# Moving the first batch's down products of a pair ahead of the second batch's transposes on TensorE, in place of ten filling products

## The chip, the cores and the metric

The kernel runs on one core of a Trainium2 chip. The metric is the device time of one execution in microseconds, lower being better: 1347.7 us as the median of three runs (1347.05 to 1351.74). The engines named below are TensorE (PE), VectorE (DVE), ScalarE (ACT), GpSimd (POOL) and SyncE (SP), the last of which issues most DMAs. Each engine has one instruction stream of its own and takes it in the order in which the program wrote it; the streams meet only in semaphores.

## The reference, cut to what matters

The model has two layers over 4 batches of 512 tokens of 256 values. Layer 0 is a local attention block with a feed-forward part, then a mixture of experts with a shared expert. Layer 1 is a slot attention of three rounds with a second mixture of experts. The change is in the shared expert and the routing of layer 0:

```
# layer 0, after the attention block; xn is the normalised residual x
logits = xn @ w_router.T                     # 8 experts
weight, idx = top_k(softmax(logits), 2)      # two experts a token
...
sh = square(relu(xn @ ws1.T))                # 256 -> 512: "up"
shared_out = sh @ ws2.T                      # 512 -> 256: "down"
return shared_out + moe_out                  # added to x through a gate
```

## The kernel before, in words

**Stages.** The first stage (layer 0 up to its experts) works on the four batches in two pairs. Inside a pair the batches 0 and 1 (then 2 and 3) are interleaved; the suffix of a step's name is the batch's place in its pair, and with it the half of PSUM (four banks each) and the set of buffers that it uses. After both pairs come the grouped experts of layer 0, then slot attention, then the experts of layer 1.

**What sets the order.** `ORDER_A` (lines 48 to 56) lists, for each engine by itself, the steps of one pair. `stages_a` (line 292) yields them for pair 0 and pair 1; a small replacement changes the beginning of pair 0 only. Nothing reorders them. At the end of a pair the steps are:

- `xnT`: PE turns (transposes) the normalised rows `S2` into banks 2 and 3 (`turn_xn`, line 1474; 8 transposes, L1461). ACT copies them to the high part of `RT` (L924), DVE makes the low part (L1103).
- `logits`: PE multiplies by the router's weights (6 products, L206 to L208; three products stand for one multiplication of split numbers). ACT's `lt` copies the logits out (L928), PE's `lt` turns them (L1487), and DVE's `logits` is `choose` (line 1105): the largest, the softmax, the best two experts. In the middle of `choose` DVE waits for the exponential on ACT (L932); that is ACT's step `logits`.
- `upA`, `upB`: PE computes the four blocks of 128 hidden rows of the shared expert. ACT takes each through Relu (L980) and Square (L982), and the square counts `sh_sq`.
- `rank`: PE sums how many earlier tokens chose each expert (L1493, L1494), DVE's `place` (line 1153) turns that into the row of destination (`dest`, L1166).
- `down`: PE waits for all four squares of the batch, then makes 16 products into banks 2 and 3 (L1612; each is recorded as two). DVE adds the result to `X` (L1303) and counts `batch_a`. On POOL `down` is `scatter` (line 802): eight indirect DMAs (L807) that write the tokens' rows to the experts' areas as soon as `dest` is there, and for batches 0 and 1 also the loading and splitting of expert weights (L469, L477). On SP it stores `X`, loads the next residual and, before the first of pair 1, runs `first_group_in` (line 429), which waits for the table of groups, three fills with zeros and every scatter.

ACT's list is `xnT0 lt0 upA0 logits0 upB0 xnT1 ...`; so the last two Relu and Square of the first batch stand behind the exponential of `logits0`. DVE's list is `... ffn1 logits0 xnT1 rank0 logits1 rank1 table1 down0 down1`; `ffn1` is the second normalisation chain of the second batch, which gives the rows that `xnT1` turns.

**Filling products.** `spin` (line 1464) issues products of constants into a bank that is free (L1467). Their results are read by nobody. Ten stand at the head of the second batch's `xnT`, ten at the head of `rank0`, six or four at the head of `logits`.

Of the kernel before, what the change touches and what calls it, by code (L numbers as in the profile page):

```python
# [46 lines left out]

ORDER_A = {
# [7 lines left out]
}  # L56
# [46 lines left out]
def build(nc, x, ctx_in, cols, rows, wq, wk, wv, wo, pos_bias, w1, w2, router1, m1_w1, m1_w2, ws1, ws2,  # L103
          Wq, Wk, Wv, wih, whh, router2, gate_w, up_w, down_w, down_b, out):
    top = ExitStack()
    with top:
# [5 lines left out]
        def sem(name):  # L112
            if name not in sems:
                sems[name] = top.enter_context(nc.semaphore(name))
            return sems[name]
# [78 lines left out]
        def bank(h, k):  # L194
            return PS[:, 4 * h + k, :]
# [1260 lines left out]
        def _(pe):  # L1456
# [7 lines left out]
            def spin(free, n):  # L1464

                for _ in range(n):
                    pe.matmul(free.rearrange("p (a b) -> p a b", b=P), ones_bf[:], ones_bf[:].unsqueeze(1).to_broadcast([P, TT, P]),  # L1467
                              start=True, stop=True)

            def parts(t, *at):  # L1470
                return tuple(t[(slice(None), i) + at] for i in two)
# [33 lines left out]
            for stage, n, h in stages_a("pe"):  # L1505
                if stage == "turn":
                    if n < 2:
                        spin(bank(h, 3), (16, 4)[n])
                    pe.wait_ge(sem("emb"), n + 1)
                    if n >= 2:  # L1510
                        pe.wait_ge(sem("dest"), n - 1)
                    turn(h, 0, EMB[h], "inT_ps")
                elif stage == "qk":
                    if n == 0:
                        spin(bank(0, 3), 8)
                        after(pe, "w3_split")
                    if n >= 2:
                        pe.wait_ge(sem("batch_a"), n - 1)
                    pe.wait_ge(sem("inT_lo"), n + 1)
                    for w in range(2):  # L1520
                        for c in range(C):
                            for c2 in range(C):
                                ins = product(pe, bank(h, 2 * w + c), parts(W3, w, c2, slice(c * P, (c + 1) * P)),
                                              parts(RT[h], c2), c2 == 0, c2 == C - 1)
                        ins.then_inc(sem("qk_ps"), 1)
                elif stage == "ewT":
                    pe.wait_ge(sem("ek"), 1)
                    pe.wait_ge(sem("ekv"), 1)
                    after(pe, "ew")
                    for jc in range(TT):  # L1530
                        for i in range(TT):
                            ins = pe.transpose(bank(0, jc)[:, i * P:(i + 1) * P], band[:, i, jc * P:(jc + 1) * P], ident[:])
                    once(ins, "ewT_ps")
                elif stage == "v":
                    pe.wait_ge(sem("th"), n + 1)
                    for j in range(TT):
                        for c in range(C):
                            ins = product(pe, token_banks(h, 0)[:, j], parts(RT[h], c, slice(j * P, (j + 1) * P)),
                                          parts(W3, 2, c), c == 0, c == C - 1)
                    ins.then_inc(sem("v_ps"), 1)  # L1540
                    pe.wait_ge(sem("ekT"), n + 1)
                    for j in range(TT):
                        for c in range(C):
                            ins = pe.transpose(token_banks(h, 2)[:, j, c * P:(c + 1) * P], S0[h][:, c, j * P:(j + 1) * P], ident[:])
                    ins.then_inc(sem("ek_ps"), 1)
                elif stage in ("den", "num"):

                    pe.wait_ge(sem("ek" if stage == "den" else "ekv"), n + 1)
                    if n == 0:
                        after(pe, "ewT")  # L1550
                    b, src = (2, 0) if stage == "den" else (0, 2)
                    w = HB[h][:, src:src + 2].rearrange("p b (a d) -> p (b a) d", d=D)
                    for c in range(C):
                        for j in range(TT):
                            ins = pe.matmul(bank(h, b + c), w[:, j, c * P:(c + 1) * P], EWT[:, j], start=j == 0, stop=j == TT - 1)  # L1555
                    ins.then_inc(sem(f"{stage}_ps"), 1)
                elif stage == "attn":
                    if h == 0:
                        pe.wait_ge(sem("ekv"), n + 2)
                        spin(bank(1, 0), 8)  # L1560
                    pe.wait_ge(sem("yT"), n + 1)
                    if n == 0:
                        pe.wait_ge(sem("wplain_in"), 48)
                    for j in range(TT):
                        for c in range(C):
                            ins = pe.matmul(token_banks(h, 0)[:, j], HB[h][:, 4 + c, j * P:(j + 1) * P], WO[:, c], start=c == 0, stop=c == C - 1)
                    ins.then_inc(sem("attn_ps"), 1)
                elif stage == "aT":
                    pe.wait_ge(sem("r_norm"), n + 1)
                    turn(h, 2, S2[h], "aT_ps")  # L1570
                elif stage == "hid":
                    spin(bank(h, 0), 10)
                    pe.wait_ge(sem("aT_lo"), C * (n + 1))
                    for m in range(HC):
                        if m >= 4:
                            pe.wait_ge(sem("hidden"), HC * n + m - 3)
                        for c in range(C):
                            ins = product(pe, bank(h, m % 4), parts(W1, c, slice(m * P, (m + 1) * P)), parts(RT[h], c), c == 0, c == C - 1)
                        ins.then_inc(sem("hid_ps"), 1)
                elif stage == "ffn":  # L1580
                    pe.wait_ge(sem("hidden"), HC * (n + 1))
                    for j in range(TT):
                        for m in range(HC):
                            ins = pe.matmul(token_banks(h, 0)[:, j], HB[h][:, m, j * P:(j + 1) * P], W2[:, m], start=m == 0, stop=m == HC - 1)  # L1584
                    ins.then_inc(sem("ffn_ps"), 1)
                elif stage == "xnT":
                    if h == 1:
                        spin(bank(h, 2), 10)
                    turn_xn(0, n, h, "xn")
                elif stage == "logits":  # L1590
                    spin(bank(h, 0), (6, 4)[h])
                    logits(0, n, h)
                elif stage == "lt":
                    logits_by_token(0, n, h)
                elif stage in ("upA", "upB"):
                    for f in (0, 1) if stage == "upA" else (2, 3):
                        if f >= 2:
                            pe.wait_ge(sem("sh_relu"), SC * n + f - 1)
                        for c in range(C):
                            ins = product(pe, bank(h, 2 + f % 2), parts(WS1, c, slice(f * P, (f + 1) * P)), parts(RT[h], c), c == 0, c == C - 1)  # L1600
                        ins.then_inc(sem("sh_ps"), 1)
                elif stage == "rank":
                    if h == 0:
                        spin(bank(1, 0), 10)
                    ranks(0, n, h)
                elif stage == "table":
                    table_pe(pe, 0)
                elif stage == "down":
                    pe.wait_ge(sem("sh_sq"), SC * (n + 1))
                    for j in range(TT):  # L1610
                        for f in range(SC):
                            ins = pe.matmul(token_banks(h, 2)[:, j], HB[h][:, f, j * P:(j + 1) * P], WS2[:, f], start=f == 0, stop=f == SC - 1)  # L1612
                    ins.then_inc(sem("shared_ps"), 1)
# [177 lines left out]
```

## Time and profile before

| what | value |
|---|---|
| median of three runs | 1347.7 us |
| the profiled execution: its own time | 1333.26 us |
| its span, first to last instruction | 1331.5 us |
| PE, DVE, ACT, POOL busy | 85%, 56%, 29%, 27% of the span |
| mean granted TensorE clock | 0.947 of full speed |

The first stage is the time up to about 361 us. Pair 0 ends for PE near 190.5 us, pair 1's PE work near 359 us, and the experts of layer 0 start on PE at 361.55 us. The profiled execution took 14.4 us less than the median of the timed runs; a change is read as a difference inside the profiled execution and then set on the median.

### The profile page before, as it was taken

The numbers are of one execution on the slowest core, as the hardware profiler recorded it, in microseconds if no ns is written. First come the engines' busy times: TensorE is split into PE (matmuls) and PEld (weight loads), VectorE is DVE, ScalarE is ACT, GpSimd is POOL, SyncE is SP. The second block draws the span as 40 slices with busy tenths as digits, with TensorE's granted clock in tenths as the row PEclk, the third lists the DMA queues.
The fourth block names the chain that finished last, engine by engine and source line by source line (L and its number), as shares of the span: only waits on it lengthen the run. The fifth ranks groups of instructions, "written<-read, shape, count | busy, mean of one in ns | idle before, by whom it ended". The sixth has DMA issues, their size and how long they took to land.

```text
span 1331.5 us, 17144 instructions
## 1 busy us (share of the span) xinstructions
PE 1125.3 (85%) x5915; PEld 882.1 (66%) x5915; DVE 742.3 (56%) x1778; ACT 385.3 (29%) x705; POOL 356.8 (27%) x290
## 2 busy tenths in 40 slices
PE   7989899898778677999999679999998299998930
PEld 5467676576667644787878447868784199998930
DVE  5565745657555435646555545454547366665633
ACT  3122221222234332233332333332332033332310
POOL 2423162231422161410101320101012523305235
PEclk9999999999999987999999999999999599999975
DMA  9401041000376650200000110000003854444435
GB/s 340 167 1 32 1 149 58 1 0 1 130 225 201 195 167 4 60 0 0 1 1 1 48 48 0 0 1 0 1 1 118 262 157 144 149 150 144 141 109 175
DMA packets 90833, 112.60 MB, mean 85 GB/s; under 512 B 6544, under 2 KB 76432, under 8 KB 90640
## 3 DMA queue, kind: packets, MB, share of 16 engines
q1 hardware_dynamic: 66800, 71.91, 16.7%
q0 software_dynamic: 19344, 34.35, 8.7%
q10 hardware_dynamic: 4624, 5.51, 1.3%
q8 instruction: 37, 0.61, 0.2%
q14 instruction: 28, 0.23, 0.1%
HBM read 75.04 MB, written 36.70 MB: 84 GB/s over the span
## 4 chain that ended last, share of the span: by engine, by line
PE 53%; DVE 18%; POOL 9%; issue 8%; ACT 5%; DMA 5%; SPq 2%; ACTq 0%; POOLq 0%; DVEq 0%
PE PS L206 12%; PE PS L208 10%; PE PS L207 10%; PE PS L1694 6%; PE PS L1584 4%; PE PS L1555 4%; POOL routed L807 4%; POOL HB L866 2%; DVE S L1099 2%; POOL rstd L800 2%; DVE st L1080 1%; PE PS L1461 1%; DVE SM L1379 1%; DMA outputs<-y 1%; DVE RT L1103 1%
## 5 line engine op out<-in xcount | busy, mean ns | idle before, releaser
L800 POOL TENSOR_TENSOR rstd<-ve,minus_half 128x4 f32<-128x4 f32 x40 | 40.6, 1015 | 359.3 <-DVE ve L1087 208.2
L206 PE MATMUL PS<-xt,split 128*128 128x256 f32 x412 | 121.2, 294 | 15.6 <-issue 12.5
L1467 PE MATMUL PS<-ones_bf 128*128 128x512 bf16 x433 | 114.2, 411 | 19.1 <-DMA routed<-S,dest 16.3
L207 PE MATMUL PS<-xt,split 128*128 128x256 f32 x412 | 119.2, 289 | 0.0
L208 PE MATMUL PS<-xt,split 128*128 128x256 f32 x412 | 119.0, 289 | 0.0
L477 POOL TENSOR_TENSOR split<-raw,split 128x1024 fp32r<-128x1024 f32 (+1 forms) x15 | 66.7, 4443 | 121.8 <-DMA raw<-down_w 73.1
L206 PEld LDWEIGHTS PS<-xt,split 128*128 128x128 f32 x412 | 81.7, 198 | 19.2 <-issue 14.4
L1467 PEld LDWEIGHTS PS<-ones_bf 128*128 128x128 bf16 x433 | 43.2, 105 | 75.9 <-issue 40.4
L1694 PE MATMUL PS<-VP,HB 128*128 128x257 f32 x384 | 85.8, 382 | 4.4 <-DVE VP L1392 4.4
L206 PE MATMUL PS<-split,hs 128*128 128x256 f32 x244 | 77.5, 318 | 10.5 <-DVE hs L541 8.9
L807 POOL DMA_INDIRECT routed<-S,dest x64 | 66.5, 1040 | 67.1 <-DVE dest L1166 49.3
L1694 PEld LDWEIGHTS PS<-VP,HB 128*128 128x128 f32 x384 | 72.4, 190 | 17.5 <-DVE VP L1392 7.4
L866 POOL DMA_INDIRECT HB<-outputs,source x64 | 64.0, 1000 | 68.2 <-DMA outputs<-y 49.5
L207 PEld LDWEIGHTS PS<-xt,split 128*128 128x128 f32 x412 | 81.9, 199 | 0.0
L208 PEld LDWEIGHTS PS<-xt,split 128*128 128x128 f32 x412 | 81.8, 198 | 0.0
L520 ACT ACTIVATE act<-PS,colv 128x256 f32<-128x256 f32 x84 | 39.9, 475 | 129.2 <-PE PS L208 129.2
L556 DVE SCALAR_TENSOR_TENSOR act<-PS,colv,act 128x256 f32<-128x256 f32 x84 | 40.7, 485 | 52.7 <-ACT act L520 48.3
L207 PE MATMUL PS<-split,hs 128*128 128x256 f32 x244 | 69.5, 285 | 0.0
L208 PE MATMUL PS<-split,hs 128*128 128x256 f32 x244 | 69.4, 284 | 0.0
L206 PE MATMUL PS<-HTS,WHH 128*128 128x512 f32 x144 | 60.5, 420 | 1.5 <-DVE RT L1103 1.5
L206 PEld LDWEIGHTS PS<-split,hs 128*128 128x128 f32 x244 | 46.8, 192 | 21.3 <-DVE hs L541 20.9
L1027 ACT ACTIVATE HB<-PS,SM 128x512 f32<-128x512 f32 x48 | 33.0, 688 | 94.0 <-DVE SM L1381 93.6
(305 smaller groups left out, 2730.2 us busy)
## 6 DMA issues: line engine op xcount, KB each, us to landing
xg<-routed SPq DMA_DIRECT2D x42, 256.0 KB, 2.8
outputs<-y SPq DMA_DIRECT2D x40, 256.0 KB, 2.3
outputs<-zeros SPq DMA_DIRECT2D x3, 2048.0 KB, 16.1
routed<-zeros SPq DMA_DIRECT2D x20, 256.0 KB, 3.2
split<-m_w POOLq DMA_DIRECT2D x16, 256.0 KB, 4.8
x_base<-X SPq DMA_DIRECT2D x8, 512.0 KB, 3.4
raw<-gate_w SPq DMA_DIRECT2D x8, 512.0 KB, 6.7
raw<-up_w SPq DMA_DIRECT2D x8, 512.0 KB, 8.7
```

Of the source, the lines that this page charges most:

```text
L206: pe.matmul(out_, a[1], b[0], start=first, stop=False)
L207: pe.matmul(out_, a[0], b[1], start=False, stop=False)
L208: return pe.matmul(out_, a[0], b[0], start=False, stop=last)
L477: eng.tensor_tensor(w.split[e % 2][:, 1], w.raw[:], w.split[e % 2][:, 0].bitcast(F32), ALU.subtract).then_inc(sem(f"m{m}_lo"), 1)
L556: dve.scalar_tensor_tensor(out=a[:, 1], in0=PS[:, f, 0:G], scalar=col("gate_b", e * w.fc + f), in1=a[:, 0], op0=ALU.add, op1=ALU.mult).the ...
L800: pool.tensor_tensor(rstd[h][:], ve[h][:], minus_half[:], ALU.pow).then_inc(sem("rstd_ready"), 1)
L807: pool.indirect_dma_start(out=routed[m], out_offset=bass.IndirectOffsetOnAxis(ap=dest[m][:, n, j, kk:kk + 1], axis=0), in_=S2[h][:, j], in ...
L866: pool.indirect_dma_start(out=rows_h[h][:, kk, j], out_offset=None, in_=outputs, in_offset=bass.IndirectOffsetOnAxis(ap=source[:, n, j, kk ...
L1467: pe.matmul(free.rearrange("p (a b) -> p a b", b=P), ones_bf[:], ones_bf[:].unsqueeze(1).to_broadcast([P, TT, P]), start=True, stop=True)
L1555: ins = pe.matmul(bank(h, b + c), w[:, j, c * P:(c + 1) * P], EWT[:, j], start=j == 0, stop=j == TT - 1)
L1584: ins = pe.matmul(token_banks(h, 0)[:, j], HB[h][:, m, j * P:(j + 1) * P], W2[:, m], start=m == 0, stop=m == HC - 1)
L1694: ins = pe.matmul(bank(h, j)[:, 0:D + 1], HB[h][:, m, j * P:(j + 1) * P], VP[h][:, m, 0:D + 1], start=m == 0, stop=m == TT - 1)
```

## The change

In PE's list `down0` moves from behind `table1` to behind `upB0`, that is ahead of the turn `xnT1`. In DVE's list `down0` moves from behind `table1` to behind `xnT1`, ahead of `rank0`. The ten filling products at the head of `xnT1` are removed. The lists of ACT, POOL and SP are as they were, and the same list serves both pairs.

```diff
 ORDER_A = {
     "pe": "turn0 turn1 qk0 qk1 v0 v1 den0 num0 den1 attn0 num1 attn1 aT0 hid0 aT1 hid1 ffn0 ffn1 "
-          "xnT0 logits0 upA0 lt0 upB0 xnT1 rank0 logits1 lt1 upA1 upB1 rank1 table1 down0 down1",
+          "xnT0 logits0 upA0 lt0 upB0 down0 xnT1 rank0 logits1 lt1 upA1 upB1 rank1 table1 down1",
...
     "dve": "turn0 turn1 qk0 qk1 v0 v1 den0 num0 den1 attn0 num1 norm0 aT0 attn1 norm1 aT1 in0 ctx0 in1 ctx1 ffn0 xnT0 ffn1 "
-           "logits0 xnT1 rank0 logits1 rank1 table1 down0 down1",
+           "logits0 xnT1 down0 rank0 logits1 rank1 table1 down1",
...
                 elif stage == "xnT":
-                    if h == 1:
-                        spin(bank(h, 2), 10)
                     turn_xn(0, n, h, "xn")
```

On PE, in pair 0, behind the last product of the first batch's `upB`; L1467 is a filling product, L1610 (L1612 before) a down product, L1461 a transpose of the second batch's rows:

```order
 L207 MATMUL PS<-RT,WS 128x512
 L208 MATMUL PS<-RT,WS 128x512
-L1467 MATMUL PS<-ones_bf 128x512 x10
+L1610 MATMUL PS<-WS,HB 128x256 x16
 L1461 MATMUL PS<-ident,S 128x128 x8
 L1467 MATMUL PS<-ones_bf 128x512 x10
```

The first batch's 16 down products now stand between its last up product and the transposes, and the ten filling products are gone from there.

On PE, at the end of pair 0, behind the sums of `rank1` and ahead of the next pair's transposes of `EMB`:

```order
 L1493 MATMUL PS<-rbf,tri 128x32
 L1494 MATMUL PS<-rbf,ones_bf 128x32
-L1612 MATMUL PS<-WS,HB 128x256 x32
+L1610 MATMUL PS<-WS,HB 128x256 x16
 L1461 MATMUL PS<-ident,EMB 128x128 x16
 L206 MATMUL PS<-RT,W 128x512
```

Of the 32 down products of both batches the 16 of the second one stay.

On DVE, in pair 0, between the low part of the second batch's turned rows (L1103) and `place` of the first batch (L1159 and on); L1303 adds the down products to `X`:

```order
 L1151 COPY carry<-carry 128x8
 L1103 TENSOR_TENSOR RT<-PS,RT 128x1024
+L1303 SCALAR_TENSOR_TENSOR X<-PS,tanh_g,X 128x1024
 L1159 TENSOR_TENSOR RTM<-PS,ebase 128x32
 L1162 TENSOR_TENSOR RTM<-RTM 128x32
```

The addition now stands ahead of the instructions that give `dest` of the first batch. Pair 1 shows the same three differences.

## Rows read from the trace of the kernel before

**Rows 1.** The page: busy time by engine, and the chain that ended last by engine
```profile
PE 1125.3 (85%) x5915; PEld 882.1 (66%) x5915; DVE 742.3 (56%) x1778; ACT 385.3 (29%) x705; POOL 356.8 (27%) x290
...
PE 53%; DVE 18%; POOL 9%; issue 8%; ACT 5%; DMA 5%; SPq 2%; ACTq 0%; POOLq 0%; DVEq 0%
```

**Rows 2.** The chain of waits, 130 to 410 us: start, us, what
```profile
167.13 1.14 DVE RT L1103
168.31 0.40 PE PS L206
...
176.79 13.91 PE PS L1612 x64
190.70 0.89 PE PS L1461 x8
...
336.20 1.12 POOL routed L807
...
355.38 2.44 DMA routed<-S,dest
```

**Rows 3.** Timeline of PE, end of pair 0: start, us, engine, line, what, [idle before <-releaser]
```profile
156.85 2.33 PE L1467 MATMUL PS<-ones_bf 128*128 128x512 bf16 x10
162.11 1.71 PE L1461 MATMUL PS<-ident,S 128*128 128x128 f32 x8 [2.93 <-DVE S L1099]
...
176.34 0.40 PE L208 MATMUL PS<-RT,WS 128*128 128x512 f32 x1
...
176.64 14.06 PE L1612 MATMUL PS<-WS,HB 128*128 128x256 f32 x64
190.54 1.91 PE L1461 MATMUL PS<-ident,EMB 128*128 128x128 f32 x16
```

**Rows 4.** Timeline of ACT, end of pair 0
```profile
162.42 0.23 ACT L932 ACTIVATE RTM<-RTM 128x32 f32<-128x32 f32 x1 [7.44 <-DVE RTM L1113]
...
164.31 0.63 ACT L982 ACTIVATE HB<-HB 128x512 f32<-128x512 f32 x1
164.85 1.01 ACT L924 ACTIVATE RT<-PS 128x1024 fp32r<-128x1024 f32 x1
...
177.40 0.63 ACT L982 ACTIVATE HB<-HB 128x512 f32<-128x512 f32 x1
```

**Rows 5.** Timeline of pair 1's end: PE, DVE and ACT
```profile
328.55 1.09 PE L1461 MATMUL PS<-ident,S 128*128 128x128 f32 x8 [2.92 <-DVE S L1099]
...
334.76 0.39 PE L206 MATMUL PS<-RT,rw 128*8 128x512 f32 x1 [0.35 <-DVE RT L1103]
...
334.62 0.18 DVE L1159 TENSOR_TENSOR RTM<-PS,ebase 128x32 f32<-128x32 f32 x1
...
330.75 0.63 ACT L982 ACTIVATE HB<-HB 128x512 f32<-128x512 f32 x1
```

**Rows 6.** Timeline of PE after 8 us idle, and granted clock: window, us, PE busy, PEclk
```profile
503.96 1.97 PE L1461 MATMUL PS<-ident,S 128*128 128x128 f32 x8 [8.06 <-DVE S L1099]
...
507.00:508.00 1.00, 1.00 (x6) 0.91 0.00 0
...
1061.92:1067.00 5.08, 5.08 (x24) 0.50 0.93 324
```

**Rows 7.** The DVE line of the down result; SP's wait; PE's first transposes of the experts
```profile
L1303 DVE SCALAR_TENSOR_TENSOR X<-PS,tanh_g,X x4: 1282/1284/1285, 183.8 to 359.1; 128x1024 f32<-128x1024 f32 x4
...
SPq L437 <- DMA routed<-S,dest: 3.2, 1, 3.2
...
361.55 0.63 PE L591 MATMUL PS<-ident,S 128*128 128x128 f32 x4 [2.48 <-DMA S<-routed]
```

**Rows 8.** Timeline of POOL and DVE at the start of pair 1
```profile
205.86 4.74 POOL L828 TENSOR_TENSOR EMB<-EMB,rowv 128x1024 f32<-128x1024 f32 x2
...
206.72 1.56 DVE L1239 TENSOR_TENSOR kb<-kb,colv 128x2 f32<-128x2 f32 x1
208.31 2.31 DVE L1241 TENSOR_TENSOR kb<-colv,kb 128x2 f32<-128x2 f32 x1
```

## The prediction, made before the changed kernel was run

> **What bounds the kernel now.** I read the page first. PE is busy 85% of the span and holds 53% of the chain that ended last [rows 1], so PE work that goes from the chain could pay. But these are means over stages, so the next view is the chain of waits over the first stage [rows 2]. There the two pairs end in different ways. In pair 0 the chain runs DVE (L1103), the logits at 168.31, the up products, then 13.91 us of down products, then the next pair's transposes at 190.70: the end of pair 0 is PE work. In pair 1 the chain leaves PE: from 336.20 it runs over POOL's sixteen scatters and their last landing at 357.82 (355.38 + 2.44), and the 64 records of down products are not in it. So the down products cost time in pair 0 and lie under the scatters in pair 1.
>
> Then the timeline of PE around the new place [rows 3]. Before, PE issued ten filling products at 156.85, idled 2.93 us, and turned the second batch's rows at 162.11, when DVE's normalisation gave them. About 5.3 us lie between the last up product and that turn, and a batch's down products last half of the 13.9 us from 176.64 to 190.54, 6.95 us. If they could start at 156.85, little of them would be late. So the question is when their operands are there, and that is read on ACT [rows 4]: the fourth square (L982) of the first batch ends at 164.94 (164.31 + 0.63), because ACT sat idle 7.44 us in front of the exponential L932, whose argument DVE makes only after the second batch's normalisations. In the old place nobody noticed. In pair 1 the fourth square ends at 331.38 (330.75 + 0.63) [rows 5].
>
> **The change part by part.** I sum against the profiled execution (1333.26 us, span 1331.5) and set the difference on the median, 1347.7.
>
> *The ten filling products (2.33 us in each pair) go.* They lay in PE's idle time in front of 162.11, so nothing is gained; but the idle stretch that they shortened becomes one.
>
> *down0 on PE, pair 0.* It waits for `sh_sq`, so PE stands from about 156.85 to 165.0, 8.15 us. Behind it in PE's stream are the transposes of `xnT1`, `rank0`, `logits1` and all of `upA1`, `upB1`; they wait too. The clock: after the 8.06 us idle in front of 503.96 the eight transposes took 1.97 us where the warm ones of 328.55 took 1.09, and the granted clock was at 0.50 (1.2 GHz) until it rose just behind 507.0, about 3.1 us of work; the longest stretch of that kind is 5.08 us at 0.50 [rows 5, 6]. I take 3.9 us of cold work, between the two, which does the work of half that time: +1.95 us, bounded by +1.55 and +2.55. So down0 takes 6.95 + 1.95 = 8.9 us and ends at 173.9, where before the transposes began at 162.11.
>
> From there to the logits: eight transposes warm, 0.9 us to the next instruction (190.70 has 0.89 [rows 2]); ten filling products of `rank0`, 2.33; the two sums, 0.1; four filling products, 0.93: 4.25 us, so the logits start at 178.15. The other way, ACT's copy 1.03 and DVE's low part 1.23 after the transposes, gives 177.2 and is shorter. Before, they started at 168.31: +9.85. The up products follow without a gap as before, so the last one, at 176.34, starts at 186.2.
>
> *The tail of pair 0.* down1 now is the first product after up. Its last square ended at 178.03 (177.40 + 0.63) [rows 4], hidden under down0's products; it now ends at 187.9, and PE waits some 1.4 us for it. Then 6.95 us: the next pair's transposes start at 194.85 instead of 190.54. Pair 0 costs **+4.3 us**: 9.85 later, 6.95 shorter, 1.4 of new wait.
>
> *Pair 1.* The same, from the fourth square at 331.38: down0 from 331.45 to 340.35, transposes to 341.3, ACT's copy to 342.4, DVE's low part to 343.65. In DVE's stream down0 (1.28 [rows 7]) comes next and then `place`, which began at 334.62 and now begins at 344.95: +10.3 us for the first `dest` and for the first scatter (336.20 to 346.5). The logits move from 334.76 to 344.6, +9.85, so the second batch's `dest` is 9.85 late; its eight scatters start 10.2 us after the first ones (fifteen steps from 336.20 to 355.38 are 1.28 each) and `dest` is there in time. All sixteen scatters, their landing, SP's reads of the first groups and PE's first expert transposes at 361.55 shift by 10.3. The shorter tail of PE is worth nothing: before, PE ended at 359 and idled 2.48 us [rows 7]. The table, and with it the fills, move by 9.85; SP waited 3.2 us for the last scatter after them [rows 7], so they stay hidden. Pair 1 costs **+10.3 us**. Bounds of these two terms together, from the cold stretch: 4.3 + 10.3 with -0.4 to +0.6 each.
>
> *POOL's displacement, start of pair 1.* The first scatters of pair 0 also start about 10.3 later; behind them in POOL's stream stand its split of the second expert's weights, which had some 3 us of slack in a wait for a load, and then L828. Before, L828 lay over two tiny DVE instructions, which took 1.56 and 2.31 us [rows 8] instead of about 0.16, and held ACT's exponentials. DVE's come 4.3 us later now, POOL's split and L828 some 7 us later, so the split and the first L828 lie over the two: about 2.0 + 2.3 instead of 3.9, **+0.5 us**, between -1 and +3.
>
> The Trainium skill (GPSIMD Engine Reference, section Specifications) states that GpSimd shares its SBUF interfaces with VectorE and that this hurts DVE instructions with two SBUF inputs or in a two-port mode. L1239 and L1241 have two SBUF inputs, and rows 8 agree. By that rule the moved L1303, which reads one input from PSUM, is safe wherever POOL works; its four instances spread only from 1282 to 1285 ns [rows 7], one of them beside a POOL split. By the rule the term stays near +0.5; without it I would keep the same range.
>
> *Sum:* 4.3 + 10.3 + 0.5 = +15.1 us, 1333.3 to 1348.4 in a profiled execution, and 1347.7 + 15.1 = 1362.8 in the timed runs.
>
> **The rivals.**
>
> *A, the squares are in time.* If the exponential did not hold ACT, the third and fourth squares would end near 158.3, one Relu and one Square behind the last up product. down0 would run 158.3 to 165.3 warm and the transposes be 3.2 us late. The low part was waiting for DVE's `choose` until 167.04 anyway, the logits would start near 169.5 (+1.2), and pair 0 would end 1.2 + 1.4 - 6.95 = -4.3. In pair 1 the first `dest` would be 2.8 late (1.5 from the turn, 1.28 from L1303), the total -1.5: **1346**, not slower. It decides from the point where ACT's fourth square ends before about 160. For it: 5.3 us of nearly free PE time. Against it: the 7.44 us wait of ACT [rows 4], and ACT's list is unchanged.
>
> *B, the scatters' delay is taken up before the experts.* Only pair 0 pays: 1347.7 + 4.3 = **1352**. Against it: SP waited for the last landing, and PE for SP's first read [rows 7]; the table's own shift of 9.85 less the 3.2 of slack would still leave 6.6.
>
> *C, the clock stays at 0.50 through all of down0.* Then it takes 13.9 us and each pair pays 5.0 more: 1362.8 + 10.0 = **1373**. Against it: after the same idle the clock was back after 3.1 us of work [rows 6], and down products ran densely at full speed in 176.64 to 190.54.
>
> *D, POOL's work falls worse on DVE,* for instance over three instructions that hold ACT or PE: +3 to +5 on top, **1367**. For it: rows 8 show 3.5 us lost to such a fall, and POOL's work moves by another distance than DVE's.
>
> **How the numbers follow.** Forecast 81%, A 4%, B 5%, C 4%, D 6%. The likeliest gives 1362.8, its own range 1359 to 1367 (cold stretch, POOL, and 0.1 to 0.2% of spread in the medians). The range reaches down toward B and up past D: 1355 to 1369. About 0.5%, 6.7 us, is what a measurement of this kernel can tell from no change: above 1354.4 is slower. Forecast, C and D are slower (91%); A and B are within (8%, leaving a little of B's upper side); 1% for a gain that no case shows.
>
> **What would show it.** Right: PE idle about 8 us in front of the down products in both pairs, released by ACT L982; a granted clock of 0.50 for their first 3 to 5 us; the second batch's transposes near 174 and 341; an idle of about 1.4 us in front of down1; the first scatter of pair 1 near 351 (346.5 plus pair 0's 4.3), and the first expert transposes about 15 us after 361.55. From there to the end the stretch lasts as before. Wrong: down0 starting near 158 (A); a scatter delay that doesn't reach the experts (B); down0 records still 0.44 us apart at its end (C); long tiny instructions on DVE near 211 with PE waiting behind them (D).

## The result

The changed kernel took 1356.9 us (median of 4 executions) against 1347.4 us for the kernel before on the same chip: a ratio of 1.0077, 95% interval 1.0056 to 1.0098, that is 7.5 to 13.2 us slower with its middle at +10.4. Timed a second time on another chip it took 1345.9 against 1333.5: 1.0082, 1.0051 to 1.0113, +10.9 us. The forecast was +15.1 us, 1362.8, in a range of 1355 to 1369. The time lies in the range, 5.9 us under the forecast, and the direction and the mechanism were right. The forecast itself lies above the first interval and at the upper end of the second (+15.1).

The two chips matter for reading the traces. The executions of the kernel before lie 9 to 13 us apart, lowest to highest, on one chip. But the chip of the first timed runs needs about 1347 us for it (the slower chip below), and two others 1333.4 (the quick ones). The first profiled execution, 1333.26, is of the second kind by its time. I return to this where the stages are added up.

### The profile page after: what moved, and what is told of

Its sections match the earlier page's. It is cut to its first block, busy times and chain, and to the rows that moved or that the text cites. A ratio compares the mean times of both kernels' runs of the same rounds, so it can differ in the third digit from the quotient of the medians.

```text
span 1353.5 us, 17104 instructions
## 1 busy us (share of the span) xinstructions
PE 1123.8 (83%) x5895; PEld 881.5 (65%) x5895; DVE 737.4 (54%) x1778; ACT 385.7 (28%) x705; POOL 356.5 (26%) x290
## 3 DMA queue, kind: packets, MB, share of 16 engines
q0 software_dynamic: 19344, 34.35, 8.7%
## 4 chain that ended last, share of the span: by engine, by line
PE 44%; DVE 15%; another core or an unknown queue 13%; issue 8%; POOL 7%; DMA 6%; ACT 5%; SPq 2%; POOLq 0%; DVEq 0%; ACTq 0%
PE PS L206 10%; PE PS L208 9%; PE PS L207 9%; PE PS L1692 6%; POOL routed L807 2%; PE PS L1584 2%; POOL HB L866 2%; PE PS L1555 2%; POOL rstd L800 1%; DVE SM L1379 1%; DVE S L1099 1%; PE PS L1610 1%; PE PS L1467 1%; DMA outputs<-y 1%
## 5 line engine op out<-in xcount | busy, mean ns | idle before, releaser
L206 PE MATMUL PS<-xt,split 128*128 128x256 f32 x412 | 120.3, 292 | 14.8 <-issue 11.7
L1467 PE MATMUL PS<-ones_bf 128*128 128x512 bf16 x413 | 110.8, 415 | 20.2 <-DMA routed<-S,dest 15.5
L206 PEld LDWEIGHTS PS<-xt,split 128*128 128x128 f32 x412 | 80.6, 196 | 18.9 <-issue 13.7
L1467 PEld LDWEIGHTS PS<-ones_bf 128*128 128x128 bf16 x413 | 41.3, 105 | 75.0 <-issue 42.0
L207 PEld LDWEIGHTS PS<-xt,split 128*128 128x128 f32 x412 | 80.8, 196 | 0.0
L208 PEld LDWEIGHTS PS<-xt,split 128*128 128x128 f32 x412 | 80.8, 196 | 0.0
```

The source lines that it names most:

```text
L206: pe.matmul(out_, a[1], b[0], start=first, stop=False)
L207: pe.matmul(out_, a[0], b[1], start=False, stop=False)
L208: return pe.matmul(out_, a[0], b[0], start=False, stop=last)
```

## The profile after

Timeline of PE at the end of pair 0, changed kernel (1355.3 us), with the columns of [rows 3]:

```profile
162.84 9.39 PE L1610 MATMUL PS<-WS,HB 128*128 128x256 f32 x32 [8.01 <-ACT HB L982]
172.07 1.04 PE L1461 MATMUL PS<-ident,S 128*128 128x128 f32 x8
172.95 2.32 PE L1467 MATMUL PS<-ones_bf 128*128 128x512 bf16 x10
...
185.78 7.17 PE L1610 MATMUL PS<-WS,HB 128*128 128x256 f32 x32 [1.29 <-issue]
192.80 1.91 PE L1461 MATMUL PS<-ident,EMB 128*128 128x128 f32 x16
```

The first row answers the question of the prediction: PE stood 8.01 us and was released by ACT's Square L982. Ten filling products ran in that place before [rows 3]. Behind the wait the down products took 9.23 us to the next instruction, the transposes came at 172.07, and a second, new wait of 1.29 us stands in front of down1, until ACT's last square (it ends at 185.73). This execution was 2.14 us earlier than the first trace at `xnT0` (143.77 against 145.91; the difference arises before the changed place), so its 162.84 is the 165.0 of the prediction.

Timeline of ACT there:

```profile
160.27 0.23 ACT L932 ACTIVATE RTM<-RTM 128x32 f32<-128x32 f32 x1 [7.45 <-DVE RTM L1113]
160.41 0.58 ACT L980 ACTIVATE HB<-PS 128x512 f32<-128x512 f32 x1
161.02 0.63 ACT L982 ACTIVATE HB<-HB 128x512 f32<-128x512 f32 x1
161.55 0.58 ACT L980 ACTIVATE HB<-PS 128x512 f32<-128x512 f32 x1
162.16 0.63 ACT L982 ACTIVATE HB<-HB 128x512 f32<-128x512 f32 x1
```

The third and fourth square follow the exponential directly, as in [rows 4]; the up products had been ready since 154.8. The granted clock of the stretches from the idle time on (window, us, PE busy, PEclk):

```profile
154.83:162.80 7.97, 0.00 (x1) 0.64 0.00 0
162.84:166.50 3.66, 3.65 (x9) 0.50 0.02 4
162.84:172.07 9.23, 9.22 (x32) 0.75 0.01 2
167.00:168.00 1.00, 1.00 (x6) 0.81 0.00 0
```

The clock fell to its lower level, 1.2 GHz, inside the idle stretch and came back between 167 and 168; down0 paid 9.23 - 7.0 = 2.2 us for it.

Pair 1 in the changed kernel, timelines of PE, DVE, POOL and again PE:

```profile
333.51 9.39 PE L1610 MATMUL PS<-WS,HB 128*128 128x256 f32 x32 [8.00 <-ACT HB L982]
342.74 1.04 PE L1461 MATMUL PS<-ident,S 128*128 128x128 f32 x8
...
344.87 1.23 DVE L1103 TENSOR_TENSOR RT<-PS,RT 128x1024 fp32r<-128x1024 f32 x1 [9.23 <-ACT RT L924]
346.01 1.27 DVE L1303 SCALAR_TENSOR_TENSOR X<-PS,tanh_g,X 128x1024 f32<-128x1024 f32 x1
348.32 0.17 DVE L1166 CAST dest<-RTM 128x8 int32<-128x8 f32 x1
...
348.79 1.12 POOL L807 DMA_INDIRECT routed<-S,dest  x1 [19.63 <-DVE dest L1166]
...
378.59 1.08 PE L591 MATMUL PS<-ident,S 128*128 128x128 f32 x4 [12.14 <-DMA S<-routed]
```

POOL waited 19.63 us for `dest` where it waited about 9 before, and PE waited 12.14 us for the first rows of the experts. The 2.48 us of [rows 7] are from a quick chip, and so is this row of the changed kernel, run again (1345.7 us):

```profile
376.12 1.09 PE L591 MATMUL PS<-ident,S 128*128 128x128 f32 x4 [10.31 <-DMA S<-routed]
```

PE's own work ends 49.4 us behind `xnT0` of pair 1 there, against 46.7 in the kernel before. So the late turn costs PE more than its shorter tail gives back, and what the tail gave back turned into idle time, because the chain through DVE and SP became longer still.

Which branch of that chain ends last differs between the chips. The wait that ended last for SP in front of the first group, behind its wait for the table, changed kernel, on the quick chip and on the slower one:

```profile
SPq L437 <- DMA routed<-S,dest: 4.6, 1, 4.6
SPq L416 <- DMA routed<-zeros: 1.6, 1, 1.6
```

On the quick chip the last scatter ends last, as the prediction has it. On the slower one the fills with zeros do: SP is released from its wait for the table only some 2.4 us after DVE has written it, and the fills land behind the scatters. The kernel before shows the same 1.6 us for the fills on that chip. The delay passes on by either way, since the change moves the table by 9.4 us on the quick chip and 9.8 on the slower one, nearly as much as the first scatter.

**Stage by stage.** Each column is one execution; the times are differences between two rows of its timeline. The first and the last column are from chips of the quick kind, the middle ones from the slower one.

| stretch, us | before (1333.3) | before, again (1350.9) | changed (1355.3) | changed, again (1345.7) |
|---|---|---|---|---|
| first turn `xnT0` of pair 0 to the turns of the next pair | 44.63 | 44.62 | 49.03 | 49.03 |
| to `xnT0` of pair 1 | 121.83 | 124.87 | 121.64 | 121.59 |
| from there to the first scatter | 23.83 | 23.82 | 34.35 | 34.39 |
| from `xnT0` of pair 1 to the first expert turn | 49.18 | 53.85 | 64.15 | 59.73 |
| from there to PE's last instruction | 915.97 | 925.75 | 920.89 | 913.88 |

Pair 0 costs 4.4 us (forecast 4.3) and the first scatter comes 10.5 to 10.6 us later (forecast 10.3). Behind `xnT0` of pair 1 the experts begin 10.3 us later on the slower chip and 10.55 on the quick ones. Two things in the table have nothing to do with the change. On the slower chip the way from the first scatter to the experts takes some 4.5 us more than on the quick ones. This is so in the unchanged kernel too, where DVE, PE and SP stood still in the same few us, released by nothing that the profile names. Timelines of DVE, PE and SP, kernel before run again:

```profile
359.18 0.42 DVE L676 TENSOR_TENSOR HB<-HB 128x256 f32<-128x256 f32 x1 [3.46 <-remote]
...
361.31 7.05 PE L1612 MATMUL PS<-WS,HB 128*128 128x256 f32 x17 [1.76 <-issue]
...
361.27 2.46 SPq L426 DMA_DIRECT2D routed<-zeros  x3
```

The other is the 3.0 us more of the second row, 124.87 against 121.83, and they are the clock. Timeline of PE and granted clock at one place of pair 1's attention, in the kernel before run again and in its first trace:

```profile
248.61 6.73 PE L1566 MATMUL PS<-WO,HB 128*128 128x256 f32 x16 [2.77 <-DVE HB L1259]
248.61:254.61 6.00, 6.00 (x14) 0.50 0.00 0
...
248.57 3.72 PE L1566 MATMUL PS<-WO,HB 128*128 128x256 f32 x16 [2.77 <-DVE HB L1259]
248.57:252.20 3.63, 3.63 (x17) 1.00 0.00 0
```

The same instructions stand behind the same 2.77 us of idle time. In one execution the clock fell to 1.2 GHz and stayed there for some 6 us, in the other it stayed at 2.4 GHz. The stretch of some 915 us behind the first stage varies too, by 5 to 6 us between executions of the changed and unchanged kernels on chips of one kind.

## The experiments

Each but the first was timed in up to five rounds against the kernel before on the same chip: the changes in one pair and the squares ahead of the exponential on the slower chip, the others on quick ones. Ratios are given with their 95% intervals. The edits in one pair, those of the squares and the clock, and the late addition are shown against the changed kernel; the delays, ACT's order alone and the products cut to fit against the kernel before.

### The kernel before, once more

No edit.

> The kernel before, unchanged, run and profiled once more. The first profiled execution took 1333.3 us while the timed runs had a median of 1347.4. If the 14 us between them is spread that any execution can have (stalls outside the changed place), this one differs from 1333 by several us and its stages differ in places that have nothing to do with the change; if the executions are alike, it reads 1331 to 1335 again. Every theory of the change expects its ends of pair 0 and pair 1 as in the first trace: fourth squares at 8.1 us behind the last up product, second batch's transposes about 5.3 us behind it, and the first scatter of pair 1 about 146 us behind the transposes that open pair 1.

It took 1350.9 us, so the first trace was not typical of the timed chip. The changed place is the same to 0.1 us (second column above, first and third row). The 3.0 us inside the attention of pair 1 are the clock, as shown above, and 4.7 us stand in front of the experts. Differences between traces are therefore trusted here only inside a stage and between executions of one kind of chip.

### The change in pair 0 alone

```diff
+                if pair == 1 and engine == "pe":
+                    order = order.replace("upB0 down0 xnT1", "upB0 xnT1").replace("table1 down1", "table1 down0 down1")
+                if pair == 1 and engine == "dve":
+                    order = order.replace("xnT1 down0 rank0", "xnT1 rank0").replace("table1 down1", "table1 down0 down1")
...
+                    if h == 1 and n // 2 == 1:
+                        spin(bank(h, 2), 10)
```

> The change in pair 0 alone; pair 1 keeps the old order with its ten filling products. Theory (the down products wait for squares that ACT makes late, and hold the PE stream): pair 0 costs 9.9 us at the logits, gives 7 back at its end and adds 1.4 us of a new wait, so +4.4 us over the kernel before. Rival 1 (pair 0's end is PE work and the shift is worth what the tail saves): -5 to -7 us. Rival 2 (only the chain through the scatters counts): 0.

Ratio 1.0032 (1.0013 to 1.0051): +4.3 us, 1.8 to 6.9. The trace has 48.77 us where the kernel before has 44.63, +4.1. The stage that the profile called bound by PE became longer although PE had less to do in it, because 8 us of idle time were put into PE's stream. Both rivals fall.

### The change in pair 1 alone

The same edit with the pairs exchanged.

> The change in pair 1 alone; pair 0 keeps the old order. Theory: the first scatter comes 10.3 to 10.5 us later and the experts with it, nothing is given back: +10.4 us over the kernel before, and together with the other half the 15 us of the two traces. Rival (the delay of the scatters is partly taken up by slack before or in the experts, since the timed runs show 9.5 us for both pairs and the traces of the first stage 15): +5 us, PE's wait in front of the first expert transposes and in the expert loops shorter by the rest.

Ratio 1.0055 (1.0032 to 1.0078): +7.4 us, 4.3 to 10.5. The trace shows the first scatter 34.34 us behind `xnT0` (+10.5) and the experts at 63.98, which is 10.1 more than in the kernel before on the same chip. The timing allows the theory's 10.4 and the rival's 5; a delay of the scatters that costs nothing is excluded.

### ACT's squares ahead of the exponential

```diff
-    "act": "turn0 turn1 qk0 qk1 v0 v1 aT0 hid0 aT1 hid1 xnT0 lt0 upA0 logits0 upB0 xnT1 lt1 logits1 upA1 upB1",
+    "act": "turn0 turn1 qk0 qk1 v0 v1 aT0 hid0 aT1 hid1 xnT0 lt0 upA0 upB0 logits0 xnT1 lt1 logits1 upA1 upB1",
```

> The changed kernel, and ACT's list in both pairs with upB0 ahead of logits0, so that the third and fourth squares no longer stand behind the exponential. Theory: they end some 1.5 us behind the last up product, down0 follows warm, the second batch's transposes are 3.2 us late instead of 10, pair 0 ends 4.3 us earlier than before and pair 1's first scatter is 2.8 us later: -1.5 us against the kernel before, some 11 to 16 us faster than the changed kernel. Rival 1 (the cost is the lost filling products, that is a cold clock): the down products still run at 0.50 and the time stays within 3 us of the changed kernel. Rival 2 (the down products' own length in the stream is the cost, late or not): +3 to +5 against the kernel before.

This is the test of the mechanism: the down products stay where the change put them and the filling products stay away; only what they wait for comes earlier. Ratio to the kernel before 0.9975 (0.9957 to 0.9993): -3.4 us, 0.9 to 5.8 faster. Timeline of PE, pair 0:

```profile
157.21 7.17 PE L1610 MATMUL PS<-WS,HB 128*128 128x256 f32 x32 [1.35 <-ACT HB L982]
164.22 1.04 PE L1461 MATMUL PS<-ident,S 128*128 128x128 f32 x8
...
177.93 7.17 PE L1610 MATMUL PS<-WS,HB 128*128 128x256 f32 x32 [1.29 <-issue]
184.94 1.91 PE L1461 MATMUL PS<-ident,EMB 128*128 128x128 f32 x16
```

The wait is 1.35 us instead of 8.01, the products run 7.0 us at full clock, and the pair ends 40.18 us behind `xnT0` instead of 44.63: -4.45, forecast -4.3. In pair 1 the first scatter is 1.65 us later, where I had reckoned 2.8. The turn is 3.2 us late, but DVE's `choose` had held the low part L1103 before; it starts only 0.45 us later (21.56 us behind `xnT0` instead of 21.11), and L1303 adds 1.2. Both rivals fall: the lost filling products cost nothing once the operands are there, and the length of the down products in the stream is mostly hidden. One word in ACT's list turns the change from a loss of 10 us into a gain of 3.

### The clock kept up

```diff
                 elif stage == "down":
+                    if h == 0:
+                        spin(bank(1, 2), 32)
                     pe.wait_ge(sem("sh_sq"), SC * (n + 1))
```

> The changed kernel with 32 filling products (7.4 us) put ahead of down0's wait in both pairs, so that PE is not idle in the 8 us. Theory: the granted clock stays at 1.00, down0 takes 7.0 us instead of 9.2 in both pairs, nothing else moves: -2.2 us in each pair, -4.5 us against the changed kernel, +6 to +10 against the kernel before. Rival (the cost of the change is mainly the lost filling and the cold clock): back to within 2 us of the kernel before.

Ratio 1.0064 (1.0040 to 1.0088): +8.5 us, 5.3 to 11.7. Timeline of PE and granted clock:

```profile
155.06 7.08 PE L1467 MATMUL PS<-ones_bf 128*128 128x512 bf16 x32
163.21 7.17 PE L1612 MATMUL PS<-WS,HB 128*128 128x256 f32 x32 [1.07 <-ACT HB L982]
170.22 1.04 PE L1461 MATMUL PS<-ident,S 128*128 128x128 f32 x8
...
163.21:170.20 6.99, 6.99 (x32) 1.00 0.00 0
```

down0 takes 7.0 us at full clock. Pair 0 ends 46.80 us behind `xnT0` (+2.2 instead of +4.4) and the first scatter comes after 32.11 (+8.3 instead of +10.5). So the clock is worth 2.2 us in each pair, as the first stage shows it; the timing is too wide to tell -4.5 from nothing. The rest of the cost stays, and the rival falls.

### A delay of pair 1 alone

```diff
                     if h == 1:
-                        spin(bank(h, 2), 10)
+                        spin(bank(h, 2), 10 if n < 2 else 80)
```

> The kernel before with 70 more filling products (16.3 us) at the head of pair 1's second turn; no order is changed. They delay that turn from 5.3 to about 18.6 us behind the last up product, and the first scatter by 10 to 11 us, as the change does in pair 1. This measures by itself what a 10.4 us delay of pair 1's scatters costs in the timed runs. If delay passes on in full: +10 to +11 us. If some 3 us of it are given back somewhere behind the scatters (the change in pair 1 alone timed +7.4 where its trace of the first stage shows 10.3): +7 to +8.

Ratio 1.0056 (1.0038 to 1.0074): +7.5 us, 5.1 to 9.9. The eighty products ran 17.44 us, less than I had reckoned, and the first scatter and the experts came 9.25 us later. The timing's middle is 1.8 us under that and its interval holds it.

The same with 150 instead of 80:

> As the run with 70 more filling products at pair 1's second turn, with 140 more: the first stage ends 16.2 us later than there, 25.5 us later than before (9.2 + 16.2). If a delay passes on in full: +25 to +26 us. If a fixed slack of 2 to 3 us behind the first stage takes up its part once: +22.5 to +23.5. If a share of a quarter is given back: +19.

Ratio 1.0171 (1.0141 to 1.0201): +22.8 us, 18.8 to 26.8. The experts began 24.4 us later (73.61 against 49.18). The middle is 1.6 us under it. A share of a quarter, 18.3 of 24.4, is excluded; a fixed 2 us that is given back once fits, and so does nothing at all.

### ACT's order alone

The edit of ACT's list above, in the kernel before.

> The kernel before, with ACT's upB0 ahead of logits0 in both pairs and nothing else. The squares end at 6 us before anybody waits for them, so every theory of the change says 0 (within 1 us). If it gained 3 us by itself, the result of the run with the squares first would be ACT's order and not the moved down products.

Ratio 0.9986 (0.9971 to 1.0002): -1.9 us, not told from 0. In the trace pair 0 takes 44.59 us against 44.63 and the first scatter 23.83 against 23.83. Part of the 3.4 us of the run above may be this, but the stage shows nothing of it.

### The changed kernel again, and the addition put back late

> The changed kernel, unchanged, timed against the kernel before in five rounds, since the first interval (+0.56% to +0.98%) is wide and its middle, 10.4 us, lies under the 14.7 us that the traces of the first stage show (4.4 in pair 0, 10.3 in pair 1 against an execution on the same chip). If all of the delay passes on: +14 to +15 us. If some 3 us are given back behind the first stage whenever pair 1 is late: +11 to +12. If the two halves add up as timed (4.3 + 7.4): +11.7.

Ratio 1.0082 (1.0051 to 1.0113), +10.9 us; the difference of the medians is 12.4. Against the first trace, of the same kind of chip, its span is 12.4 longer: +14.6 up to the experts and -2.1 behind.

```diff
-           "logits0 xnT1 down0 rank0 logits1 rank1 table1 down1",
+           "logits0 xnT1 rank0 logits1 rank1 table1 down0 down1",
```

> The changed kernel with DVE's down0 (L1303, 1.28 us) back in its old place behind the table, PE's down0 staying in the new one. It parts the 10.3 us of pair 1: theory says that 1.15 to 1.28 of them are L1303 in front of place. First scatter of pair 1 1.2 us earlier than in the changed kernel; the time -1.2, hardly told from 0 by the timing. In pair 0 nothing changes, since PE's tail ends it. Rival (the wait of place for rank's sums, not L1303, ends last there): the scatter stays.

Timelines of DVE and POOL, pair 1:

```profile
345.12 1.22 DVE L1103 TENSOR_TENSOR RT<-PS,RT 128x1024 fp32r<-128x1024 f32 x1 [9.17 <-ACT RT L924]
346.26 0.19 DVE L1159 TENSOR_TENSOR RTM<-PS,ebase 128x32 f32<-128x32 f32 x1
...
347.86 1.12 POOL L807 DMA_INDIRECT routed<-S,dest  x1 [18.39 <-DVE dest L1166]
```

`place` follows the low part at once and the first scatter comes 33.10 us behind `xnT0`, 1.29 earlier than in the changed kernel, so the addition's share is shown in the stage. The rival, that the wait for the sums of `rank` ends last there, falls. The time did not follow: 1.0105 (1.0080 to 1.0130), +14.0 us (10.7 to 17.3). The interval overlaps that of the changed kernel; a 1.3 us step is below what these rounds can tell. Its stages sum to +13.5 (4.2 in pair 0 and 9.3 in pair 1), so here nothing is missing in the timed runs.

### Down products cut to fit the gaps

```diff
+                if pair == 0 and engine == "pe":
+                    order = order.replace("upB0 xnT1 rank0", "upB0 downA0 xnT1 downB0 rank0").replace("table1 down0 down1", "table1 down1")
+                if pair == 0 and engine == "act":
+                    order = order.replace("upA0 logits0 upB0", "upA0 upB0 logits0")
+                if pair == 0 and engine == "dve":
+                    order = order.replace("xnT1 rank0", "xnT1 down0 rank0").replace("table1 down0 down1", "table1 down1")
...
-                    for j in range(TT):
+                    for j in {"down": range(TT), "downA": (0, 1), "downB": (2, 3)}[stage]:
...
-                    ins.then_inc(sem("shared_ps"), 1)
+                    if stage != "downA":
+                        ins.then_inc(sem("shared_ps"), 1)
```

The filling products at the heads of `xnT1` and `rank0` are left out in pair 0.

> Built on the theory: in pair 0 alone ACT's squares go ahead of the exponential, and down0 is cut into two halves of eight products: one between the last up product and the second batch's turn, one behind the turn in place of rank0's ten filling products. DVE adds the result behind xnT1. Pair 1 is the kernel before. Each half is 3.5 us and fits the 3.8 us from the squares to the turn and the 4.2 us from the turn to the logits, so nothing behind is late; the tail of pair 0 loses 7.0 us and gains a wait of 1.4: -5.5 us against the kernel before. Rival (PE's stream is the bound only in this trace, DVE and ACT take its place): -1 or nothing.

Ratio 0.9954 (0.9935 to 0.9972): -6.1 us, 3.7 to 8.7 faster than the kernel before, 1326.5 against 1333.4 us. Timeline of PE, pair 0 (L1618 is a down product, L1467 here a transpose):

```profile
156.10 3.72 PE L1618 MATMUL PS<-WS,HB 128*128 128x256 f32 x16 [1.35 <-ACT HB L988]
159.88 1.09 PE L1467 MATMUL PS<-ident,S 128*128 128x128 f32 x8
160.81 3.62 PE L1618 MATMUL PS<-WS,HB 128*128 128x256 f32 x16
...
166.07 0.39 PE L206 MATMUL PS<-RT,rw 128*8 128x512 f32 x1 [0.67 <-DVE RT L1109]
...
175.84 7.17 PE L1618 MATMUL PS<-WS,HB 128*128 128x256 f32 x32 [1.29 <-ACT HB L988]
182.85 1.91 PE L1467 MATMUL PS<-ident,EMB 128*128 128x128 f32 x16
```

The logits start 22.38 us behind `xnT0` (22.40 before), and the pair ends 39.16 us behind it, 5.47 less than 44.63: the 7.0 us less the new wait of 1.3 to 1.4, with 0.1 to 0.2 left over. Both ends of the rival, -1 and nothing, are excluded. This version beats both kernels.

## Why the prediction was right, and where it was off

**The down products wait for late squares.** Shown. Forecast wait 8.15 us, measured 8.01 and 8.00, released by ACT L982; with the squares earlier the wait was 1.35 us and the loss a gain.

**Cold work.** Forecast +1.95, bounds 1.55 to 2.55; measured 2.2 in both pairs, and 0 with the idle stretch filled. Right.

**Pair 0.** Forecast +4.3, trace +4.4, timed alone +4.3 (1.8 to 6.9). Right, with its parts: the last up product starts 9.84 us later (forecast 9.85), the down products behind it are 6.88 us shorter (6.95), and the start of down1 moved 1.44 us away from the sums in front of it (1.4); the 1.29 of the timeline are the idle part of that.

**Pair 1 up to the experts.** Forecast +10.3, trace +10.5 at the scatter and +10.3 to +10.55 at the experts. The parts are measured too: 2.2 are the clock and 1.3 the addition ahead of `place`; the other 7 or so are the late turn. SP's slack of 3.2 us did cover the fills on a quick chip: it still waited 4.6 us for the last landing in the changed kernel. On the slower chip, where the change was timed first, it did not. The fills ended last there, in the kernel before too, so the 10.3 us passed on through the table and not through the scatters. The number held because the two move nearly alike.

**POOL's displacement.** Forecast +0.5, measured 0; here the step failed. The two tiny DVE instructions ran their 0.16 us at 209.02 and 209.22, since POOL's split started only at 210.82. I had let POOL's work come some 7 us later, by taking 3 us of slack out of the wait for the split's load. But POOL issues that load itself, behind its late scatters. The wait shrank only from 5.59 to 4.07 us, and the split came 9.5 us later. But that gave no gain either: from the next pair's turns of `EMB` to the second batch's `ekT` turn the changed kernel takes 21.37 us and the kernel before 21.43. PE was busy with `v` until then, so the 3.5 us that DVE lost before [rows 8] had been hidden. I priced a wait without looking at who waited for it. The trace agrees with the Trainium skill's rule as far as it goes (GPSIMD Engine Reference, section Specifications): the instructions with two SBUF inputs were short where POOL was not at work, and L1303 of the second batch took 1.29 us at 193.00 beside POOL's split. In the new place of L1303 POOL stood idle, so that place tests nothing. Timelines of POOL and DVE, changed kernel:

```profile
192.42 2.37 POOL L477 TENSOR_TENSOR split<-raw,split 128x1024 fp32r<-128x1024 f32 x1 [2.61 <-DMA split<-m_w]
...
193.00 1.29 DVE L1303 SCALAR_TENSOR_TENSOR X<-PS,tanh_g,X 128x1024 f32<-128x1024 f32 x1 [7.02 <-PE PS L1610]
```

**"From there to the end the stretch lasts as before."** This is the term of the sum that stays open. Forecast 0. The stage sums are 14.7 and 14.6 us, the timings +10.4 (7.5 to 13.2) and +10.9 (6.8 to 15.1), so about 2 to 4 us are missing behind the first stage. The pure delays miss 1.8 of 9.25 and 1.6 of 24.4, each within its interval; the change in pair 0 alone misses nothing (4.1 to 4.4 against 4.3). The change in pair 1 alone misses 2.7 (10.1 against 7.4), the run with the clock kept 2.0 (10.5 against 8.5), and the run with the addition put back late, whose experts begin late too, nothing (13.5 against 14.0). All but the last fit some 2 us that come back once when the experts begin late, and the last speaks against it. Only in the first timing of the change does the stage sum, 14.7, lie outside the interval of the time, which ends at 13.2. In the traces the stretch behind the first stage scatters by more: 911.9 to 916.5 us with early experts (three executions on quick chips) and 913.2 to 914.5 with late ones (five). There PE's busy time varies with the length, 798.5 of 912.5 us in the shortest and 803.0 of 916.5 in the first trace, for the same 4522 instructions. That is what the clock does in the attention of pair 1 above; that it is the clock here too is not shown. Which wait shrinks, if any does, I could not find.

The rivals: A, with the squares in time, was put at -1.5 and is what the run with ACT's order changed made real, at -3.4 (0.9 to 5.8 faster). B, in which pair 1 pays nothing, fell with the change in pair 1 alone; a small part given back stays open, as said. C fell by the clock rows. D fell, since no DVE instruction was held at that place.

## What to carry to other kernels

Idle time in front of an instruction is room for other work only if that work's operands exist by then; look at when its last producer ends, not at when its first one starts, and at what stands ahead of that producer in its own engine's list. A step that was harmless behind everything shows its late operands only when it is moved forward, and in an in-order stream everything behind it pays. Before paying for a hidden collision, ask who waits for it.

## What the runs showed of the hardware that was not expected

- One program takes 1333 us on two chips and 1347 on a third. Part of the difference is seen at one place: 4.5 us in front of the experts, in which DVE, PE and SP stood together (DVE 3.46 us, released by something that the profile doesn't name). All five traces from that chip, of changed and unchanged kernels, show it, and none of the eight from quick chips. The stretch behind the first stage is longer on it too, 919 to 926 us against 912 to 917. Neither cause was tried.
- After 8 us of idle time the granted clock was at 0.50 for the first 4.5 us or so of down products (162.84 to about 167.4), longer than the 3.1 us of work that I had read behind 503.96 [rows 6]; 7.1 us of filling products in the same place kept it at 1.00.
- The same 2.77 us of idle time in front of the same products (L1566 in pair 1) was followed by the lower clock in five of the thirteen traces, for about 3 to 6 us, and by the full clock in the other eight. It happened on both kinds of chip and cost 1.7 to 3.0 us. So two executions of one kernel can differ by 3 us in a stage that nobody touched.
